# Gated delta rule block plus small MoE block on one Trainium2 core: key products of two heads alternated, and unread bf16 products put in front of projections and decay broadcasts

## The reference, cut to what matters

```python
q = _causal_dwconv(x @ Wq, qcw, qcb); k = ...; v = ...     # 3 x 1024 channels, 4 taps, silu
q, k = _rope(q), _rope(k)                                  # then each divided by its norm
alpha = exp(-exp(A_log) * softplus(x @ gkw + gkb + dt_bias))   # one decay per token and head
S_new = at * (S - bt * kt (x) (kt S)) + bt * kt (x) vt         # the recurrence over tokens
ot = qt S + D * (qt . kt) * vt
```

## Time and profile before

| | |
|---|---|
| median of 3 runs | 7591.35 us |
| profiled execution | 7579.47 us, of which the span is 7577.7 us |
| mean granted TensorE clock | 0.731 of full |
| PE busy | 5724.0 us (76%), 40448 instructions |
| VectorE (DVE) busy | 4737.2 us (63%) |
| ScalarE (ACT) busy | 3028.1 us (40%) |
| GpSimd (POOL) busy | 2662.3 us (35%) |

### The profile page before, as it was taken

How to read it: one execution, slowest core, us unless ns; L and a number is a source line. 1 busy time by engine, 2 the same in 40 slices (tenths; PEclk the granted TensorE clock), 3 DMA queues, 4 the chain that set the end, 5 groups by cost and what they waited for, 6 DMA issues and landing times.

```text
span 7577.7 us, 126105 instructions
## 1 busy us (share of the span) xinstructions
PE 5724.0 (76%) x40448; PEld 4010.6 (53%) x40448; DVE 4737.2 (63%) x11688; ACT 3028.1 (40%) x5605; POOL 2662.3 (35%) x2990
## 2 busy tenths in 40 slices
PE   4777777777777777777777777787777877777777
PEld 3455554555545655545555455554555544555545
DVE  5755567655676565676556765557665567665672
ACT  2344334443344443344443444434444334443343
POOL 3433333433334332343322343323433233332341
PEclk6677776877767777677777677776777767777777
DMA  1000000000000000000000000000000000000000
GB/s 64 2 2 3 3 2 2 3 3 3 3 1 3 3 3 3 2 2 3 3 3 2 2 3 3 3 2 1 3 3 3 3 1 3 3 3 3 2 2 3
DMA packets 26461, 29.73 MB, mean 4 GB/s; under 512 B 4073, under 2 KB 22769, under 8 KB 25329
## 3 DMA queue, kind: packets, MB, share of 16 engines
q1 hardware_dynamic: 25712, 20.49, 0.9%
HBM read 16.29 MB, written 4.19 MB: 3 GB/s over the span
## 4 chain that ended last, share of the span: by engine, by line
PE 38%; issue 32%; POOL 15%; DVE 10%; ACT 3%; POOLq 1%; SPq 0%; DVEq 0%; ACTq 0%; DMA 0%
PE bank L855 38%; POOL NP L589 4%; POOL Gam L617 4%; POOL Gam L614 3%; DVE NP L1380 2%; POOL NP L586 2%; DVE NP L1247 2%; DVE hn L1233 1%; POOL NP L592 1%; PE bank L859 1%; POOL frstd L655 1%; ACT Gam L744 1%; ACT NP L690 1%; DVE Gam L1399 1%; DVE lpp L1267 1%
## 5 line engine op out<-in xcount | busy, mean ns | idle before, releaser
L855 PE MATMUL bank<-QK 64*128 64x256 f32 (+1 forms) x4096 | 1323.1, 450 | 251.5 <-ACT pT L818 100.0
L855 PEld LDWEIGHTS bank<-QK 64*128 64x128 f32 (+1 forms) x4096 | 575.6, 174 | 851.7 <-ACT pT L818 254.0
L1247 DVE SCALAR_TENSOR_TENSOR NP<-bank,conv_w,NP 128x255 f32<-128x255 f32 (+2 forms) x2304 | 929.8, 472 | 78.0 <-ACT NP L690 78.0
L842 ACT ACTIVATE QK<-bank,b 128x256 f32<-128x256 f32 x1024 | 419.7, 470 | 907.7 <-PE bank L855 906.2
L855 PE MATMUL bank<-xnT,Wqkv 128*128 128x256 f32 x1536 | 556.3, 506 | 101.2 <-DVE NP L1247 53.4
L1565 DVE SCALAR_TENSOR_TENSOR moe<-bank,wsel,moe 128x128 f32<-128x128 f32 x512 | 156.0, 347 | 755.6 <-PE bank L855 755.6
L855 PE MATMUL bank<-NP,head_cols 128*32 128x256 f32 x1536 | 209.4, 489 | 523.5 <-POOL NP L586 523.4
L855 PE MATMUL bank<-mT,W 128*128 128x256 f32 x2048 | 558.4, 424 | 0.6
L744 ACT COPY Gam<-NP 32x256 f32<-32x256 f32 x512 | 321.3, 627 | 566.7 <-DVE fac L1387 562.2
L690 ACT ACTIVATE NP<-bank,conv_b,conv_w 128x256 f32<-128x256 f32 x768 | 388.6, 556 | 344.1 <-PE bank L855 344.0
L855 PE MATMUL bank<-W,QK 128*128 128x128 f32 x4096 | 505.3, 277 | 22.5 <-DVE moe L1565 22.5
(11 more groups left out here) (212 smaller groups left out, 11312.2 us busy)
## 6 DMA issues: line engine op xcount, KB each, us to landing
xin<-in_x SPq DMA_DIRECT2D x33, 128.0 KB, 2.0
out<-moe SPq DMA_DIRECT2D x32, 128.0 KB, 2.5
W<-in_W SPq DMA_DIRECT2D x1, 2048.0 KB
NP<-in_c_q_sel SPq DMA_DIRECT2D x1, 1536.0 KB, 8.3
NP<-in_c_k_sel SPq DMA_DIRECT2D x1, 1536.0 KB, 11.5
NP<-in_c_alpha_sel SPq DMA_DIRECT2D x1, 1024.0 KB, 5.0
Wqkv<-in_Wq SPq DMA_DIRECT2D x1, 512.0 KB, 12.3
Wqkv<-in_Wk SPq DMA_DIRECT2D x1, 512.0 KB, 12.9
```

The costliest lines, as they stand in the source:

```text
L842: ins = s.activation(h1[:, n % 2, f, :], ps[:, q, :], ACT.Gelu_apprx_tanh, bias=b1[:, n, f:f + 1])
L855: return mm(out_, lhsT, rhs, start=first, stop=last)
L1247: v.scalar_tensor_tensor(acc[:, n % 2, m, j:T], ps[:, m, 0:T - j], conv_w[:, kind, c, PAD - j:KT - j], acc[:, n % 2, m, j:T], ALU.mult, AL ...
```

## The change

`bank_uses()` gives all decay broadcasts bank 4 and the key products banks h mod 4. A new helper issues n bf16 products, 128x128 by 512 columns, whose result nothing reads, into a bank just before that bank's real product overwrites it: three in front of each of the twelve rounds of projections, one in front of each of the 16 decay broadcasts. The key products of heads 2c and 2c+1 are issued together: tile 0 of the even head, tile 0 of the odd head, tile 1 of the even, tile 1 of the odd. The broadcast of head h+1 stands behind the pair that holds head h, and the pieces of the second block stand behind the broadcast.

```diff
-        g += [(("alpha", h), h % 2, "v_Gam", h + 1), (("kk", h), 2 + h % 2, "v_NP", h + 1)]
+        g += [(("alpha", h), 4, "v_Gam", h + 1), (("kk", h), h % 4, "v_NP", h + 1)]
...
+            def keep_active(ps, n):
+                for _ in range(n):
+                    product(ps[:], identb[:], q_sel[:, 0, 0:4, :].rearrange("p c k -> p (c k)"))
...
                         if reused(i, use):
                             pe.wait_ge(*free_at(i, use))
+                        keep_active(bank(use), 3)
                         ps = pair(bank(use))
...
-                for h in range(H):
-                    c, rows = h // 2, rows_of(h)
+                def decay(h):
                     if reused(i, ("alpha", h)):
                         pe.wait_ge(*free_at(i, ("alpha", h)))
                     ps = bank(("alpha", h))
+                    keep_active(ps, 1)
                     pe.wait_ge(v_alpha.sem, v_alpha.at(i, 7))
                     product(ps[:, 0:NT * GW], alpha_sel[:, h * P:(h + 1) * P],
                             alpha3[:].rearrange("p t w -> p (t w)")).then_inc(full(("alpha", h)), 1)
-                    if reused(i, ("kk", h)):
-                        pe.wait_ge(*free_at(i, ("kk", h)))
-                    ps = bank(("kk", h))
+                decay(0)
+                for c in range(NC):
+                    both = (2 * c, 2 * c + 1)
+                    for h in both:
+                        if reused(i, ("kk", h)):
+                            pe.wait_ge(*free_at(i, ("kk", h)))
                     pe.wait_ge(v_QK.sem, v_QK.at(i, c + 1))
                     for t in range(NT):
-                        ins = product(ps[:, t * T:(t + 1) * T].rearrange("p (a k) -> p a k", a=2),
-                                      QK[rows, c, 1, TOK[t]], QK[rows, c, :, TOK[t]])
-                    ins.then_inc(full(("kk", h)), 1)
-                    meanwhile(("head", h))
+                        for h in both:
+                            rows = rows_of(h)
+                            ins = product(bank(("kk", h))[:, t * T:(t + 1) * T].rearrange("p (a k) -> p a k", a=2),
+                                          QK[rows, c, 1, TOK[t]], QK[rows, c, :, TOK[t]])
+                            if t == NT - 1:
+                                ins.then_inc(full(("kk", h)), 1)
+                    for h in both:
+                        if h + 1 < H:
+                            decay(h + 1)
+                        meanwhile(("head", h))
```

## The result

The changed kernel takes 7375.76 us (median of 4 runs, 7373.6 to 7384.35) against 7604.94 us for the kernel before (4 runs); the ratio is 0.9703, with a 95% interval of 0.967 to 0.9736. That is 3.0% faster. The profiled executions differ by 7577.7 - 7382.6 = 195.1 us of span, and the medians by 229 us: the profiled execution of the kernel before (7579.5 us) was faster than all four of these runs, that of the changed kernel the slowest of its four. What follows explains the 195 us.

The account below looks back on a forecast made before the run. No engine bounds the whole; heads follow the clock, VectorE bounding at full clock, PE busy without a gap at half. Heads -4.55 and convolutions +1.45 us a batch, times 32, give -99 us: 7492 us median, range 7405 to 7635.

Parts of the forecast that it names:

- the pot: Heads: VectorE's 281 us of waiting, 8.8 us a batch, the most that changes to PE there can bring.
- three open rounds of the convolutions: Convolutions: unread products of rounds 0, 6 and 11 are not hidden, costing +0.2, +0.65 and 1.0 us a batch.
- the rest of the stage is VectorE's, so -0.4: Convolutions: a higher clock saves only 0.4 us a batch, since VectorE sets the rest of the stage.
- full clock but for one head in sixteen: Heads: added full-array work holds the full clock except in one head a batch, which costs 0.8 us.
- 3.45 us left: Heads: of 8.8 us waiting a batch, 3.45 remains, from the second scan's wait for the first pair and `rep` steps.
- VectorE starts a scan every 1.45 us without idling: it is the bound: Heads at the full clock: VectorE sets the pace, so 1.45 us a head stays after the change.
- five slots: Heads: a pair's eight key-product instructions overlap into five slots, 1.08 us at the full clock, 2.13 at the half.
- at the half clock the change is worth nothing: Heads at the half clock: unread products eat what pairing saves, 2.26 us a head against 2.32 before.
- pairing might be worth nothing at the full clock: Heads at the full clock: by the skill's PSUM rule alone, the sum of the heads would be nought.
- the slower case: Rival: the clock isn't held, heads fall to the half clock as before; +91 us, 7680 us; chance 0.12.
- The halves don't overlap: Rival, heads: a pair costs 1.72 us, its broadcast comes 0.55 us late; +24 us, 7615 us; chance 0.11.
- The products in the convolutions aren't hidden: Rival: all twelve rounds' unread products on the path, 7.8 us a batch, 7680 us; half of them 7560; chance 0.08.

Follow-up runs that it names:

- e1: Changed kernel without the unread products in front of the convolutions' projections; those in front of the broadcasts stay: 7417.11 us, ratio 0.9803.
- e7: Changed kernel with the convolutions' unread products only for rounds 1 to 5, issued behind the projection of the round before: 7322.37 us, ratio 0.964.
- e2: Changed kernel with its pairs and banks but no unread products anywhere: 7424.19 us, ratio 0.9811.
- e4: Changed kernel with both key-product tiles of a pair's even head before both of the odd head: 7383.1 us, ratio 0.9752.
- e5: Changed kernel with the same number and columns of unread products, each reading 64 rows instead of 128: 7534.37 us, ratio 0.9916.
- e3: Kernel before, with its order and banks kept and the change's unread products added: 7454.67 us, ratio 0.9849.
- e9: Changed kernel with the unread product in front of each broadcast cut from 512 columns to 128: 7398.88 us, ratio 0.9732.
- e10: Changed kernel with the even head's tiles first and one of a pair's two unread products moved between the heads' key products: 8025.2 us, ratio 1.0545.

## Why the prediction was right or wrong

**Right: the place and the price of the parts.** The heads were said to hold 281 us of VectorE's waiting as the pot, and 190 of it went. The unread product costs 0.22 us. The clock is 1.00 in the heads. The three open rounds of the convolutions were put at +1.85 us a batch, 59 us; the taps' wait grew by 70.4, all of it in these three: rounds 0, 6 and 11 by 0.58, 0.58 and 1.04 us a batch, where 0.2, 0.65 and 1.0 stood.

**Wrong, the largest miss: "the rest of the stage is VectorE's, so -0.4".** This step gave the higher clock in the convolutions 0.4 us a batch, 13 us. It is worth 76.5, and e1 and e7 show it by taking it back and keeping it. So the stage did not get 1.45 us longer, as forecast; from first tap to first scan it is 0.8 us shorter, with 0.6 more in front of the first tap. The prediction read the clock's worth off two batches at 0.75 and 0.67, which differ by 0.5 us. But in both of them `Wo` ran at the half clock (5.46 and 5.47 us for its 32 instructions) and VectorE waited 2.31 and 2.29 us for the turn behind it, so their difference could not show what a full clock there is worth. VectorE's two waits for PE's turns, 97 us in the kernel before, are a row each of the list of groups, and the sum has no term for them. They stood behind `yT` and `Wo`, just the work that a full clock shortens.

**Wrong: "full clock but for one head in sixteen", and 3.45 us left.** This gave the heads -4.55 us a batch, 146 us in all. Nearly no head was at the half clock (0.8 us a batch had been set aside, 26 us), and VectorE still waited 91.1 + 0.0 us, 2.85 a batch instead of 3.45 (another 19). The waits behind the `rep` steps were 1.01 and 0.54 us where about 1.5 and 0.65 stood in the sum. With the miss above, and less the 11 us by which the open rounds were too cheap, this is 64 + 44 - 11 = 97 us: the forecast's 99, and 196 measured in these waits.

**Wrong: "VectorE starts a scan every 1.45 us without idling: it is the bound".** In the changed kernel a scan starts every 1.40 us in the mean with the same two instructions between, and in e2 every 1.39 at the full clock. The 1.45 were not VectorE's own pace. The rows of before allow the reading that I missed: PE's key products start at 3092.62, just after the multiplication that begins at 3091.71 ends (3092.56) and frees one of their two banks. The next broadcast stands behind them and ends at 3093.96, and the scan that needs it starts at 3094.00. With four banks for the key products this ring is gone, about 0.05 us a head. This is read from the rows and was not tried by itself.

**Wrong, with hardly any effect on the sum: five slots, and no price for pairing alone.** The eight instructions take four slots, not five, because the halves run in twos from the start; and e4 shows that the alternation, on which the reasoning rested, is not needed. At the full clock the forecast had the fifth slot hidden anyway. That "at the half clock the change is worth nothing" was said of pairs and unread products together, 4.51 us a pair; the changed kernel was hardly ever at the half clock, and the nearest that was measured is e5, at 4.48 us a pair with unread products on 64 rows. What was wrong is what followed from it: the second eats what the first saves, so the clock got all the credit. Pairs without unread products take 3.52 us there (e2), and by e2 and e3 each part alone brings more than half of the gain in the heads (4.4 and 3.4 of 6.4 us).

Against pairing the prediction drew on the Trainium skill (TensorEngine Tiling (Array Packing), section PSUM Bottleneck), that tiling speeds up TensorE but not the evacuation of PSUM. It took from this that pairing might be worth nothing at the full clock. With unread products in both, e3 and the changed kernel measure that: at a clock of 1.00 the fourteenth batch's heads take 27.65 us without pairs and 26.15 with them. There PE, not the evacuation, was the bound. Without unread products the gain at the full clock is small, 1.45 to 1.39 us a head (e2), and may be the banks'.

**The rivals.** The clock was held, so the slower case did not come. In e5 and e9 it was held only in part, and both are still faster than the kernel before, by 0.8 and 2.7%. e10 is 5.5% slower where the rival had 1.2%, but it lost the overlap as well as the clock, so it does not price this rival. "The halves don't overlap" fell to a single row, eight instructions in 1.13 us. "The products in the convolutions aren't hidden" was true of the three rounds that were named, and of no others.

## What to carry to other kernels

Before pricing a higher TensorE clock, list every wait of the other engines for PE in the stretch, not only those next to the edit: the clock shortens all of them, and here the ones out of sight gave 76.5 us, as much as the added products cost in the same stage. Here products on different halves of the rows shared their time where they stood next to each other in PE's stream, in either order, and into different banks; one product on all rows between them cost the whole overlap. An unread product in front of a product that is itself waited for is paid in full and has to earn more than that through the clock. In the heads it does (about 1.2 us a batch paid, e9); in rounds 0 and 6 to 11 of the convolutions it didn't, and taking it out of there, with those of rounds 1 to 5 moved behind the projection of the round before, was worth 0.7%.

## What the runs showed of the hardware

- Matmuls on two different row halves start in twos even when the program puts four of one half before four of the other (e4: 1.14 us for eight; changed kernel: 1.13; the kernel before: 1.13 for four). PE did not keep the order of the program between the halves there, by the records' starts and by the signals of the two heads, 0.06 us apart.
- Of two sets of unread products with equal number and columns, the one on 128 rows held the fourteenth batch's heads at a clock of 1.00, the one on 64 rows left it at 0.88 (e5); cutting the columns to a quarter left 0.87 (e9).
- The same instructions, one of them moved, came with a clock of 0.64 instead of 1.00 (e10): the lost overlap cost twice here, once in PE's time and once in its clock.
